# Cross-attention and mixture-of-experts layer: the queries' product with the key bias moved from TensorE to GpSimd and VectorE

## The reference

```python
Q = hm_tokens @ Wq + bq                       # hm_tokens = layernorm(x), 16 x 256 x 128
K = text_tokens @ Wk + bk
scores = jnp.einsum('bqd,bkd->bqk', Q, K) / jnp.sqrt(jnp.float32(d))
scores = jnp.where(text_mask[:, None, :] == 0, jnp.float32(NEG), scores)
attn = jax.nn.softmax(scores, axis=-1)
x = x + attn @ V                              # V = text_tokens @ Wv + bv
...
out = sum over the two chosen experts of weight * down(u * silu(gate))
```

## Time and profile before

| | |
|---|---|
| median of 3 runs | 457.65 us (457.65 to 460.37) |
| the profiled execution's own time | 463.26 us |
| its span | 461.3 us |
| PE busy in the span | 395.5 us (86%) |
| DVE busy | 345.0 us (75%) |
| ACT busy | 268.0 us (58%) |
| POOL busy | 253.8 us (55%) |

### The profile page before, as it was taken

How to read it: one execution, slowest core, us unless ns; L and a number is a source line. 1 busy time by engine, 2 the same in 40 slices (tenths; PEclk the granted TensorE clock), 3 DMA queues, 4 the chain that set the end, 5 groups by cost and what they waited for, 6 DMA issues and landing times. The chain is left out here.

```text
span 461.3 us, 10376 instructions
## 1 busy us (share of the span) xinstructions
PE 395.5 (86%) x2742; PEld 359.3 (78%) x2742; DVE 345.0 (75%) x1453; ACT 268.0 (58%) x642; POOL 253.8 (55%) x347
## 2 busy tenths in 40 slices
PE   2598999999999999999999997488999989966940
PEld 2597999989989999999999996366888868855730
DVE  2477889889889889889889988467677747752942
ACT  1156666666566666576576655246787758753730
POOL 1072343665765756757657565477766646651650
PEclk9989999999999999999999999879999989995985
DMA  5955374275276267357447511412333643394119
GB/s 153 308 163 160 128 260 148 104 270 191 89 255 230 78 234 243 94 198 242 128 163 242 150 30 40 99 54 60 105 99 93 150 80 87 94 265 111 47 40 270
DMA packets 72216, 68.67 MB, mean 149 GB/s; under 512 B 6224, under 2 KB 64736, under 8 KB 72160
## 3 DMA queue, kind: packets, MB, share of 16 engines
q1 hardware_dynamic: 67584, 58.52, 41.3%
q0 software_dynamic: 4544, 9.38, 6.3%
q10 hardware_dynamic: 32, 0.10, 0.1%
HBM read 54.41 MB, written 13.57 MB: 147 GB/s over the span
## 5 line engine op out<-in xcount | busy, mean ns | idle before, releaser
L1254 PE MATMUL ps<-attention,ctx_sb 128*128 128x128 f32 (+1 forms) x832 | 114.1, 278 | 11.0 <-ACT attention L675 5.3
L1254 PEld LDWEIGHTS ps<-attention,ctx_sb 128*128 128x128 f32 (+1 forms) x832 | 101.5, 191 | 18.1 <-issue 11.7
L620 POOL DMA_INDIRECT parts<-mbias,blk_x x78 | 78.7, 1009 | 51.0 <-ACT mbias L742 42.8
L675 ACT ACTIVATE attention<-ps 128x512 f32<-128x512 f32 x96 | 56.5, 597 | 35.0 <-PE ps L1236 31.0
L558 POOL DMA_INDIRECT rows_in<-kept,place x64 | 67.8, 1059 | 14.5 <-issue 12.8
L521 POOL TENSOR_TENSOR rstd<-ve,minus_half 128x2 f32<-128x2 f32 x32 | 26.8, 836 | 86.0 <-DVE ve L865 86.0
L1236 PE MATMUL ps<-ident,attention 128*128 128x128 f32 (+1 forms) x416 | 67.5, 278 | 0.0
L809 DVE CUSTOM_DVE_ANT_0 attention<-ps,mbias 128x1608 f32<-128x1608 f32 x32 | 58.6, 1830 | 4.0 <-issue 4.0
L649 ACT ACTIVATE attention<-attention,ebias 128x1601 f32<-128x1601 f32 x32 | 52.0, 1624 | 10.6 <-DVE ebias L827 10.4
L1158 DVE SCALAR_TENSOR_TENSOR ctx_sb<-ctx_sb,ps 128x256 f32<-128x256 f32 x78 | 32.7, 420 | 29.9 <-ACT ctx_sb L729 29.7
L1220 PE MATMUL ps<-ctxt_high,gt_high 128*128 128x402 f32 x128 | 48.3, 377 | 5.0 <-DVE ctxt_low L951 3.0
(11 more groups left out here) (132 smaller groups left out, 850.4 us busy)
## 6 DMA issues: line engine op xcount, KB each, us to landing
ctxt_in<-ctx_cols SPq DMA_DIRECT2D x16, 800.5 KB
mbias<-mbias_dram SPq DMA_DIRECT2D x16, 800.5 KB, 5.8
ctx_sb<-ctx_rows SPq DMA_DIRECT2D x16, 768.0 KB
blk_x<-rows_in SPq DMA_DIRECT2D x78, 65.0 KB, 1.9
attention<-parts SPq DMA_DIRECT2D x16, 256.0 KB, 5.2
x_in<-x SPq DMA_DIRECT2D x16, 128.0 KB, 4.9
wup_in<-w_up_t SPq DMA_DIRECT2D x8, 256.0 KB, 5.3
out<-base_all SPq DMA_DIRECT2D x8, 256.0 KB, 4.1
```

The source lines that it names most:

```text
L620: pool.indirect_dma_start(parts, bass.IndirectOffsetOnAxis(ap=blk_x[:, m % XR, D:D + 1].bitcast(I32), axis=0), blk_y[:, m % YR], None).the ...
L675: act.activation(probs_t[:, g * BANK:(g + 1) * BANK], ps_turn[:, g % 2], ACT.Copy).then_inc(s_pt_act, 1)
L1254: last = pe.matmul(ps_o[:, 0:P], ctx_sb[0:n, j, t], probs_t[0:n, t * P:(t + 1) * P], start=t == 0, stop=t == KT - 1)
```

## The change

Wq bk is worked out once as a row that stands in all 128 partitions (wqbk_rows), by a PE product with the bias column broadcast as weights. For each batch POOL multiplies the normalised queries xn1 with that row, 128 x 256 elements, into xn1_wqbk, whose last column of each half holds bq.bk. DVE sums each half with a `tensor_reduce` over 129 elements into qbk. The four passes of PE in `prep_gt` and DVE's L795 are gone. The functions of both engines are called `query_bias`. xn1 is overwritten only when the product that reads it is made.

```diff
@@ -117,7 +117,9 @@
 
         wqt_sb = sb("wqt_sb", [P, D])
         wqk_sb = sb("wqk_sb", [P, D])
-        side_sb = sb("side_sb", [P, 3])
+        side_sb = sb("side_sb", [P, 1])
+        wqbk_rows = sb("wqbk_rows", [P, D])
+        xn1_wqbk = sb("xn1_wqbk", [P, QT, D + 1])
         wkt_sb = sb("wkt_sb", [P, D])
         wv_sb = sb("wv_sb", [P, D])
         wr_sb = sb("wr_sb", [P, E])
@@ -304,7 +306,8 @@
         s_ebias = sem("ebias_ready")
         s_gth = sem("gt_high_copied")
         s_gtc = sem("gt_split")
-        s_qbk = sem("qbk_copied")
+        s_qbk = sem("qbk_ready")
+        s_qprod = sem("qbk_products_made")
         s_pt_dve = sem("probs_t_by_dve")
         s_rsum = sem("rsum_ready")
         s_x1 = sem("x1_ready")
@@ -497,8 +500,18 @@
                 wait(pool, s_xn1, 2 * i + j)
                 pool.tensor_tensor(rstd1[:], ve1[:], minus_half[:], ALU.pow).then_inc(s_rs1, 1)
 
+            def query_bias(b):
+
+                j = b % 2
+                pool.wait_ge(s_xn1, b + 1)
+                wait(pool, s_qbk, b)
+                pool.tensor_tensor(xn1_wqbk[:, :, 0:D], xn1[:, j], wqbk_rows[:].unsqueeze(1).broadcast_to([P, QT, D]),
+                                   ALU.mult).then_inc(s_qprod, 1)
+
             def slot_first(i, k):
                 u = 4 * i + k
+                if k % 2 == 0 and is_unit(u + 2):
+                    query_bias(u // 2 + 1)
                 if is_unit(u - 2):
 
                     pool.wait_ge(s_y, u - 1)
@@ -569,6 +582,8 @@
                                pattern=[[-1, P]], channel_multiplier=1).then_inc(s_ident, 1)
             pool.tensor_copy(iota_f[:], iota_i[:]).then_inc(s_iota, 1)
             rstd_of_x(0, 0)
+            pool.wait_ge(s_wqkc, 1)
+            query_bias(0)
             rstd_of_x(0, 1)
 
 
@@ -778,6 +793,7 @@
                 dve.wait_ge(s_rs1, b + 1)
 
                 wait(dve, s_xt, b - 1)
+                wait(dve, s_qprod, b - 1)
                 for t in range(QT):
                     last = dve.tensor_scalar(xn1[:, j, t], x_in[:, j, t], mv1[:, t, 0:1], rstd1[:, t:t + 1],
                                              ALU.subtract, ALU.mult)
@@ -791,11 +807,17 @@
                 wait(dve, s_scores, QT * (b - 1))
                 dve.tensor_scalar(gt_high[:, j], ps_misc[:, 0:SQ], side_sb[:, 0:1], None, ALU.add).then_inc(s_gth, 1)
 
-                wait(dve, s_ebias, QT * (b - 1))
-                dve.tensor_scalar(qbk[:, j], ps_misc[:, SQ:SQ + QT], side_sb[:, 2:3], None, ALU.add).then_inc(s_qbk, 1)
                 dve.wait_ge(s_gth, b + 1)
                 dve.scalar_tensor_tensor(gt_low[:, j], ps_misc[:, 0:SQ], side_sb[:, 0:1], gt_high[:, j].bitcast(F32),
                                          ALU.add, ALU.subtract).then_inc(s_gtc, 1)
+
+            def query_bias(i, j):
+
+                b = 2 * i + j
+                dve.wait_ge(s_qprod, b + 1)
+
+                wait(dve, s_ebias, QT * (b - 1))
+                dve.tensor_reduce(qbk[:, j], xn1_wqbk[:], AX.X, ALU.add).then_inc(s_qbk, 1)
 
             def maximum(i, k):
 
@@ -998,6 +1020,8 @@
                 if is_unit(u - 2):
                     take_logits(i, k - 2)
 
+                if k % 2 == 1 and is_unit(u + 1):
+                    query_bias(*((i, 1) if k == 1 else (i + 1, 0)))
                 if is_unit(u + 1):
                     maximum(*following)
                 if is_unit(u - 2):
@@ -1061,11 +1085,14 @@
 
             dve.wait_ge(s_wqk, 1)
             dve.tensor_copy(wqk_sb[:], ps_misc[:, 0:D])
-            dve.tensor_copy(side_sb[:], ps_misc[:, D:D + 3]).then_inc(s_wqkc, 1)
+            dve.tensor_copy(wqbk_rows[:], ps_misc[:, D:2 * D])
+            dve.tensor_copy(xn1_wqbk[:, :, D], ps_misc[:, 2 * D + 1:2 * D + 2].broadcast_to([P, QT]))
+            dve.tensor_copy(side_sb[:], ps_misc[:, 2 * D:2 * D + 1]).then_inc(s_wqkc, 1)
             ln1(0, 0)
             dve.wait_ge(s_pad, 3)
             prep_gt(0, 0)
             split_ctxt(0, 0)
+            query_bias(0, 0)
             maximum(0, 0)
             bias_sum(0, 0)
             bias(0, 0)
@@ -1200,11 +1227,7 @@
             def prep_gt(i, j):
                 b = 2 * i + j
                 pe.wait_ge(s_xtc, b + 1)
-                pe.matmul(ps_misc[:, 0:SQ], wqk_sb[:], xt_sb[:], start=True, stop=True)
-                for t in range(QT):
-                    last = pe.matmul(ps_misc[:, SQ + t:SQ + t + 1], xt_sb[:, t * P:(t + 1) * P], side_sb[:, 1:2],
-                                     start=True, stop=True)
-                last.then_inc(s_gt, 1)
+                pe.matmul(ps_misc[:, 0:SQ], wqk_sb[:], xt_sb[:], start=True, stop=True).then_inc(s_gt, 1)
 
             def score(i, k):
 
@@ -1304,9 +1327,9 @@
                     times_ctx(i, k, 3)
 
             pe.matmul(ps_misc[:, 0:D], wqt_sb[:], wkt_sb[:], start=True, stop=True)
-            pe.matmul(ps_misc[:, D:D + 1], wkt_sb[:], bq_col[:], start=True, stop=True)
-            pe.matmul(ps_misc[:, D + 1:D + 2], wqt_sb[:], bk_col[:], start=True, stop=True)
-            pe.matmul(ps_misc[:, D + 2:D + 3], bq_col[:].broadcast_to([P, P]), bk_col[:], start=True,
+            pe.matmul(ps_misc[:, D:2 * D], bk_col[:].broadcast_to([P, P]), wqt_sb[:], start=True, stop=True)
+            pe.matmul(ps_misc[:, 2 * D:2 * D + 1], wkt_sb[:], bq_col[:], start=True, stop=True)
+            pe.matmul(ps_misc[:, 2 * D + 1:2 * D + 2], bq_col[:].broadcast_to([P, P]), bk_col[:], start=True,
                       stop=True).then_inc(s_wqk, 1)
 
             pe.wait_ge(s_wqkc, 1)
```

## The result

The changed kernel takes 467.88 us (median of 4 runs, 466.90 to 470.11), the kernel before 458.19 (457.65 to 460.37) beside it: a ratio of 1.0209, with a 95% interval of 1.0159 to 1.0260, 9.7 us slower. The forecast was no change, 457.6, and the range ended at 461.5.

The account below looks back on a forecast made before the run. DVE was taken to end the even slots, PE the odd. Terms -1.55 (gt_high's start), 0 (L795), 0 (reduction), +1.8 (product in three slots), -0.3 (before the loop) gave -0.05 us: 457.6 us, range 453.5 to 461.5.

Parts of the forecast that it names:

- What bounds the loop: Unit loop: DVE comes last in the even slots, PE sets the pace in the odd, with 0.46 us DVE idle.
- The passes' worth: Even slots: earlier gt_high start gains 1.55 us, 0.07 in each of 13 slots and 0.65 in the first two.
- L795 at nothing: Even slots: removing L795 gains 0, since gt_low waits for gt_high anyway; bounds 0 and 1.9 us gained.
- The reduction: Odd slots, ahead of the maximum: DVE's 422 ns fit in its 0.46 us idle before L966; cost 0.
- Rival C: Odd slots overflow: reduction held beside POOL's L490, 3.2 us lost, 460.8 us; chance 0.10.
- The product in slots 2, 4 and 6: POOL's product holds DVE's L879 for 0.6 us in each of three slots, 1.8 us lost; bounds 0 and 2.6.
- The product in the steady slots: POOL's product waits behind DVE's split L951 in place of the sum L505; cost 0.
- rival B: Product gets the shared path ahead of L951 in 11 even slots, 0.6 us lost each, 464.2 us; chance 0.08.
- Rival A: Even slots bound by PE's stream: the whole 8.0 us and 0.3 come off, 449.3 us; chance 0.10.

Follow-up runs that it names:

- before, 128 columns behind: Kernel before plus a plain GpSimd sum of 128 columns in a spare tile behind the sum into base_all, even slots from 6; even slot 9.61 us.
- before, 128 columns ahead: Kernel before plus a plain GpSimd sum of 128 columns in a spare tile ahead of the sum into base_all; even slot 9.62 us.
- half of the product: Changed kernel, from batch 1 on only one half of the product made, the other left stale; even slot 9.88 us.
- sum first, then product: Changed kernel with the product moved behind the sum into base_all; 465.67 against 461.35 us for the kernel before, ratio 1.0092.
- changed, iota ahead of the scatter: Changed kernel with the iota moved ahead of the odd slot's second scatter; 467.95 against 459.83 us for the kernel before, ratio 1.0162.
- before with the product alone: Kernel before plus GpSimd's product at the change's place, result unused, four passes kept; 472.35 against 461.35 us, ratio 1.0214.
- the kernel before with other addresses: Kernel before plus one unused buffer, so later tiles lie as in the changed kernel; even slot 9.34 us, no ratio given.

## Why the prediction was wrong

- **What bounds the loop**: right. The even slots end with DVE, the odd ones with PE. Without the passes the even slots are 0.12 shorter and PE waits for the rest of its 0.50.
- **The passes' worth**: the mechanism right, the size somewhat small. The term was 0.07 a slot from 4 to 28; from 8 to 28 it measured 0.12 on the mean (9.34 to 9.22 in slot 18), since L808 follows L938 by 0.07 and not by 0.12 as gt_low followed the small instruction L795, and gt_low follows 0.02 sooner. A kernel without the passes gains 4.1 us by its medians (2.4 to 5.0 by the interval), where 1.55 and 0.65 were counted; the first 0.55 before slot 0's copy and the even slots from 2 to 30 give 2.6.
- **L795 at nothing**: nearly. gt_low starts 0.50 behind gt_high where it was 0.52.
- **The reduction**: right. It takes 418 ns (422 forecast), the odd slots are 7.42 us before and after, and alone it gives a ratio of 0.9995. It uses 0.22 of the 0.46 idle, not 0.42: it starts 0.08 behind the logits' copy (which takes 0.17) and lets the maximum start 0.35 behind itself, so that copy and maximum are 0.43 apart where they were 0.18. Rival C did not come: the reduction ran wholly beside GpSimd's two L493 (the L490 of before) and was not the longer for it:

```profile
155.90 0.87 POOL L493 TENSOR_TENSOR x<-x_in,bv_rows 128x128 f32<-128x128 f32 x2
...
156.35 0.42 DVE L820 TENSOR_REDUCE qbk<-xn_wqbk 128x2 f32<-128x258 f32 x1
```

- **The product in slots 2, 4 and 6**: right in kind. L901 takes 0.75 in slot 2, where it was 0.35, and ends with the product (41.52 against 40.71 + 0.74 = 41.45):

```profile
40.77 0.75 DVE L901 TENSOR_SCALAR y<-x,mv,rstd 128x128 f32<-128x128 f32 x1
...
41.65 2.11 DVE L973 TENSOR_TENSOR ctxt_low<-ctxt_in,ctxt_high 128x1601 fp32r<-128x1601 f32 x1
```

  The split behind it is longer too, 2.11. In slot 6 L901 is held although its record is the first, by 0.04:

```profile
73.77 0.86 DVE L901 TENSOR_SCALAR y<-x,mv,rstd 128x128 f32<-128x128 f32 x1
73.81 0.74 POOL L508 TENSOR_TENSOR xn_wqbk<-xn,wqbk_rows 128x256 f32<-128x256 f32 x1
```

  Beside the kernel without the passes, slots 2, 4 and 6 are 8.96, 9.30 and 9.63 against 8.76, 8.87 and 9.11: 0.2, 0.4 and 0.5, 1.15 us where 1.8 was forecast.
- **The product in the steady slots**: this is the step that failed: "So in the steady slots the product costs nothing." It rested on L951's start of 0.20 ahead of the time at which POOL is free, and on the sum's having waited there. The product alone costs 0.90 in each of these slots. It is rival B in its effect, 464.2 forecast with a chance of 0.08, but not by its condition: the order of the recorded starts did not change, the split is still the first by 0.03. B took 0.6 a slot for it, and that was too little. The whole product counts, and the gap ahead of it: in the kernel before the split could go when the cast had ended, 1.06 behind the scatter's start; now it goes when the product has ended, at 1.97 (1.22 to its start and 0.75). That is 0.91, and 0.95 at the split's end, less the 0.12 gained. The cast's greater length is no term of it.
- **Rival A**: did not come; PE's wait for the copy grew.

The ends in slot 18, in us behind the start of the scatter ahead of the cast, tell it for eight of the kernels. "First" is the GpSimd instruction behind the iota, where it ran at its own length and was not itself held:

| kernel | first ends | cast ends | split ends |
|---|---|---|---|
| before | | 1.06 | 2.72 |
| before, 128 columns behind | | 1.35 | 3.02 |
| before, 128 columns ahead | | 1.35 | 3.02 |
| half of the product | 1.69 | 1.41 | 3.39 |
| sum first, then product | 1.71 | 1.73 | 3.40 |
| changed, iota ahead of the scatter | 1.83 | 1.12 | 3.52 |
| changed | 1.97 | 1.27 | 3.67 |
| before with the product alone | 1.98 | 1.28 | 3.67 |

In the first three the split ends 1.66 or 1.67 behind the cast, in the others 1.69 or 1.70 behind the GpSimd instruction.

What is shown: the product alone makes the loss; the split ends 1.69 or 1.70 behind the end of the GpSimd instruction that is in first, whether that is the product, half of it or the sum; and beside the maximum the product costs nothing that could be measured. What stays open is by what rule an instruction gets in first. The cast's length changes with columns that GpSimd executes only later by its records. That GpSimd claims the shared path ahead of its recorded starts would fit this, but it is not shown, and I have no account that gives all of the cases: half a product ahead of the sum got in first, 128 plain columns at the same place did not. The half product stands in the changed kernel, waits on semaphores and reads two tiles; the plain columns stand in the kernel before, wait on none and read one tile twice. Which of these sets them apart was not tried.

## What to carry to other kernels

Work that is moved to GpSimd goes beside VectorE instructions that the traces show to be let alone, here a maximum out of PSUM (1.83 us with and without it) and a `tensor_reduce` (0.42), and not beside a long one with two SBUF inputs: the same product cost 0.90 us a slot at one place and nothing two instructions further on. That an instruction reads a single tile of SBUF does not save it: L901, a `tensor_scalar`, was held to 0.75 and 0.86 where it took 0.35. That a GpSimd instruction has lost such a meeting until now says nothing of the one that takes its place; price the meeting from the time at which VectorE could go to the newcomer's end, and move it if the price is not nil. And an engine's busy share says little of a step's worth: four passes of 0.50 us gave 0.12 a slot, for the other engine came last.

## What the hardware showed that was not expected

- A split of two SBUF inputs with a recorded start 0.03 us ahead of the GpSimd product's ended 1.70 us behind the product's end, as if held for the whole of it. In slot 2 of the kernel before the order was the other way: the sum's record was 0.04 ahead, and it was the sum that took 2.17. So with records this close the recorded starts do not tell who is held. The Trainium skill ("SBUF — State Buffer", section "Who interferes with whom") has the issue order decide who blocks whom, and the hold last a whole instruction. The second the traces bear out, 1.69 or 1.70 us from the GpSimd instruction's end to the split's; the first they can't show, as the records of start go against it in the changed kernel.
- A cast of four columns took 0.17 us with GpSimd idle beside it, as the timeline of the kernel before shows in slot 6:

```profile
75.25 0.17 DVE L1100 CAST place<-place_f 128x4 int32<-128x4 f32 x1
75.32 1.83 DVE L951 TENSOR_TENSOR ctxt_low<-ctxt_in,ctxt_high 128x1601 fp32r<-128x1601 f32 x1
...
75.72 2.51 POOL L558 DMA_INDIRECT rows_in<-kept,place  x1 [0.47 <-DVE place L1100]
```

  It took 0.33 beside the scatter of the steady slots, and 0.41, 0.46 and 0.61 as 2, 32 and 128 plain columns stood behind the next sum in GpSimd's row. With the product's 256 columns there it took 0.99, but then the sum had come first and the cast ended with it. A memset of two columns there added nothing. In the same three rows the scatter (L558) comes 0.40 after the split and takes 2.51 us where its median is 1.04: it ends 1.08 after the split's end (78.23 against 77.15), as if it had begun only then. So a scatter seems to be held by the split too; no run tried it by itself.
- The granted clock fell to 0.58 in slot 31 of the kernel before with other addresses, and stayed at 1.00 in the kernel before, which does the same work: 9.69 us against 8.08. PE had been busy for 0.55 and for 0.95 of the 2 us before.
